# A state-space and experts layer on one core: five states' products on GpSimd in place of seven

## The chip, the cores and the metric

The kernel runs on one core of one Trainium2 chip. The metric is the device time of one execution in microseconds (us); less is better. A verdict compares medians of several executions.

The engines are named as the profile names them: PE is TensorE's matmul side and PEld its weight loads, DVE is VectorE, ACT is ScalarE, POOL is GpSimd, SP is SyncE. On-chip memory is SBUF; the matmul results stand in PSUM, 128 partitions in both.

## What is computed

The input x holds 16 samples of 512 tokens with 128 features, in float32. Four blocks follow each other, each with a layer norm ahead of it and a residual sum behind: a Mamba block, a product-key experts block, a small gated recurrence, and the experts block again. The change lies in the Mamba block. There, with 256 inner channels d and 16 states n, every token t does

```
dA = exp(delta[t, d] * A[d, n])
h[d, n] = dA * h[d, n] + (delta[t, d] * u[t, d]) * B[t, n]
y[t, d] = sum over n of h[d, n] * C[t, n]
```

The experts block looks up 8 rows of a table for every token, takes a dot product of each with the token, a GELU, and a weighted sum.

## The kernel before, in words

**Stages.** One sample is worked on at a time in three overlapping stages: PRE of sample i+1 (layer norm, convolution, delta), CORE of sample i (the 16 states), and POST of samples i-1 and older (the rest of the Mamba block, both experts blocks and the recurrence). An iteration has 64 slots (`TURN`), four for each state: the slots 4n to 4n+3 are those of state n. Every engine walks through the same slots in program order. Beside the states, the stages of PRE and POST are put into slots by the table `SLOTS` (L57), which was written out by hand; an engine does what its slot holds and waits on semaphores where an operand is not there.

**One state in CORE.** PE spreads row n of C over all partitions into the PSUM tile `c_ps` (L767) and row n+1 of B into `b_ps` (L758), both in the first slot of state n, C first. DVE scans along the tokens (L1352): it reads the decays `dA` from SBUF, which ACT made three states earlier (L1026), and the fed values from PSUM, and writes the state to one of the four buffers `hp`. Then DVE multiplies du by `b_ps` (the feed of state n+1, L1336). The state is then multiplied by C in place. For most states DVE does this in the third slot, with `c_ps` as its second operand (L1362). For the states in `POOL_STATES` POOL does it in the first slot (L1481). It cannot read PSUM, so ACT first copies `c_ps` to the SBUF tile `c_row` (L1043), of which there is one (`NCR` is 1). PE sums the product over the states in `ysum` (L783): two multiplications by the identity for each state, which the trace shows as four records.

**What the table of states also sets.** `SUM_AT` (L225) is the state in whose first slot PE sums state n: n+1 for a DVE state, n+2 for a POOL state, at most 15. The sums stand behind the spreads of C and B in that slot. `c_used` (L609) is what frees `c_ps` for the next C: for a POOL state ACT's copy, for a DVE state DVE's product. PE waits for it in `spread_c` (L761). Behind `spread_c` in PE's order stands `spread_b`, which the next feed on DVE waits for. A scan waits until the sum of the state that used its buffer is done (L1349).

**Other work around the change, by slot.** On PE: the two large convolutions (L809) in slots 15 and 19, the two plain ones (L812) in slots 25 and 27, a layer-norm product (`pe_ln_c`) in 16, the experts' sums (L716) in 25, 34, 45 and 59, the experts' similarities (L679) in 35, 38, 44, 46, 49, 51, 54 and 56. On DVE: the experts' dot products (L1265, eight in one group) in slots 11, 16, 22, 32, 36, 44, 53 and 59, the experts' weights `coef` (L1272) in 8, 21, 35 and 51, the maxima and masks (L1232, L1239) and the indices (L1248 to L1257), the first of them in slot 42. On POOL: indirect fetches of expert rows (L1466), four to a part, in slots 9, 10, 16, 25 (three parts), 35, 36, 43 and 47 (two parts each), 61 and 62. In POOL's program a product comes ahead of the fetches of its slot.

```python
POOL_STATES = (1, 3, 5, 7, 9, 11, 13)
DVE_STATES = tuple(n for n in range(NS) if n not in POOL_STATES)
SUM_AT = [min(n + 1 + (n in POOL_STATES), NS - 1) for n in range(NS)]
```

Of the kernel before, what the change touches and what calls it, by code (L numbers as in the profile page):

```python
# [218 lines left out]
}  # L219


POOL_STATES = (1, 3, 5, 7, 9, 11, 13)
DVE_STATES = tuple(n for n in range(NS) if n not in POOL_STATES)

SUM_AT = [min(n + 1 + (n in POOL_STATES), NS - 1) for n in range(NS)]  # L225
SUM_ORDER = sorted(range(NS), key=lambda n: (SUM_AT[n], n))
# [29 lines left out]
def at(b, per, k=0):  # L256

    return b * per + (k + 1)
# [30 lines left out]
def build(nc, A):  # L289
    with ExitStack() as ctx:  # L290
# [312 lines left out]
        def multiplied(c, n):  # L603

            if n in POOL_STATES:
                return pool_read, at(c, len(POOL_STATES), POOL_STATES.index(n))
            return read_out, at(c, len(DVE_STATES), DVE_STATES.index(n))

        def c_used(c, n):  # L609

            if n in POOL_STATES:
                return c_kept, at(c, len(POOL_STATES), POOL_STATES.index(n))
            return multiplied(c, n)
# [953 lines left out]
```

## Time and profile before

| what | value |
| --- | --- |
| median of 3 executions | 2184.6 us |
| lowest, highest | 2182.73, 2188.92 us |
| the profiled execution | span 2189.7 us, its own time not listed beside it |
| busy share of PE, DVE, ACT, POOL | 77%, 81%, 70%, 62% |

The span is the time from the first to the last instruction of the one execution that was profiled. Busy time of an engine counts its data instructions, not waits, branches and semaphore work. An instruction that starts and then cannot get its operands counts as busy: its duration in the trace is longer than that of others of its kind. Square brackets behind an instruction in a timeline give the idle time of its engine ahead of it and what ended it. Not all matmul records of `c_ps` are in the trace.

### The profile page before, as it was taken

To read this page: it belongs to the slowest core of one execution; us is meant where nothing else is said; L and a number is where in the kernel's file an instruction comes from. 1 tells how busy PE (TensorE), PEld (TensorE's weight loads), DVE (VectorE), ACT (ScalarE), POOL (GpSimd) and SP (SyncE) were. 2 spreads that over 40 slices of the span, in tenths; PEclk is the share of its full clock that TensorE was granted. 3 is DMA by queue.
4 is the path that set the end of the run, shared out by engine and by line. 5 is a ranking of instruction groups with operands and counts; after the bars stand their busy time and mean duration, and the time that the engine had idled before them with its cause. 6 is when DMAs were issued, how large, how long until landed. Compare 5 with 4: busy or idle time off the path is not lost. (4 is left out here: it accounts for less than half of the span.)

```text
span 2189.7 us, 24718 instructions
## 1 busy us (share of the span) xinstructions
PE 1681.9 (77%) x6097; PEld 937.5 (43%) x6186; DVE 1767.2 (81%) x4204; ACT 1543.5 (70%) x3276; POOL 1355.7 (62%) x1209
## 2 busy tenths in 40 slices
PE   4887878787887978888888879788878877754562
PEld 2332435354544545454544444454544444433342
DVE  3898989798988989898898989898889997733331
ACT  4565868587877868787878778777877765554542
POOL 0226463667776667677676676677677776566554
PEclk8898989998999999998999989999989988886776
DMA  2001120222222222222222222322222222233222
GB/s 54 0 10 56 32 65 23 62 66 75 82 80 77 70 84 68 82 77 65 84 80 77 73 84 68 84 68 74 76 75 82 72 80 73 71 87 92 78 82 71
DMA packets 79901, 151.06 MB, mean 69 GB/s; under 512 B 20584, under 2 KB 46592, under 8 KB 79680
## 3 DMA queue, kind: packets, MB, share of 16 engines
q0 software_dynamic: 49152, 134.28, 21.3%
q1 hardware_dynamic: 29344, 14.65, 2.4%
q8 instruction: 61, 1.00, 0.2%
q14 instruction: 96, 0.79, 0.1%
q10 hardware_dynamic: 1248, 0.34, 0.1%
HBM read 145.01 MB, written 4.19 MB: 68 GB/s over the span
## 5 line engine op out<-in xcount | busy, mean ns | idle before, releaser
L1466 POOL DMA_INDIRECT rows<-in_experts,index x1024 | 980.8, 958 | 477.6 <-issue 363.2
L1352 DVE TENSOR_TENSOR_SCAN hp<-dA,fed_ps 128x1024 f32<-128x1024 f32 x256 | 582.3, 2275 | 7.0 <-issue 5.8
L783 PE MATMUL ysum<-hp,ident 128*128 128x512 f32 x1024 | 503.9, 637 | 16.0 <-DVE hp L1362 9.0
L1481 POOL TENSOR_TENSOR hp<-hp,c_row 128x1024 f32<-128x1024 f32 x112 | 263.9, 2356 | 279.2 <-ACT c_row L1043 179.8
L1336 DVE TENSOR_TENSOR fed_ps<-du,b_ps 128x1024 f32<-128x1024 f32 x256 | 313.4, 1224 | 58.4 <-remote 26.3
L1026 ACT ACTIVATE dA<-delta,decay 128x511 f32<-128x511 f32 x512 | 334.8, 711 | 15.8 <-issue 7.9
L1005 ACT ACTIVATE rows<-rows,coef 128x128 f32<-128x128 f32 x1024 | 311.0, 390 | 19.2 <-DVE coef L1272 19.2
L783 PEld LDWEIGHTS ysum<-hp,ident 128*128 128x128 f32 x1024 | 215.0, 211 | 251.3 <-issue 218.5
L1265 DVE CUSTOM_DVE_ANT_0 rows<-rows,xn 128x128 f32<-128x128 f32 x1024 | 261.5, 318 | 51.7 <-DMA rows<-in_experts,index 51.2
L933 ACT ACT_TABLE_LOAD x218 | 279.7, 1283 | 8.8 <-PEq L543 5.0
L716 PE MATMUL bank<-rows,ident 128*128 128x256 f32 x1024 | 247.4, 397 | 34.0 <-ACT rows L1005 33.4
L716 PEld LDWEIGHTS bank<-rows,ident 128*128 128x128 f32 x1024 | 206.0, 202 | 67.2 <-ACT rows L1005 34.6
L679 PE MATMUL bank<-w_sim,xnT 128*128 128x512 f32 x256 | 175.1, 773 | 70.3 <-ACT x L998 30.4
L1232 DVE TENSOR_REDUCE top<-bank 128x16 f32<-128x512 f32 x128 | 87.4, 683 | 116.2 <-PE bank L679 72.6
L1362 DVE TENSOR_TENSOR hp<-hp,c_ps 128x1024 f32<-128x1024 f32 x144 | 174.7, 1214 | 2.4 <-PE c_ps L767 0.8
L758 PE MATMUL b_ps<-split,pick 128*128 128x512 bf16 x251 | 106.4, 424 | 36.8 <-DVE fed_ps L1336 21.0
L998 ACT ACTIVATE x<-bank 128x256 f32<-128x256 f32 x64 | 24.3, 379 | 151.4 <-remote 70.8
L986 ACT ACTIVATE flip<-bank 128x1024 bf16<-128x1024 bf16 x64 | 65.1, 1017 | 84.9 <-PE bank L690 57.9
L809 PE MATMUL bank<-xrT,w_taps 128*128 128x512 f32 x256 | 118.1, 604 | 3.4 <-ACT ucs L1117 2.5
L1239 DVE TENSOR_TENSOR mask<-bank,top 128x512 bf16<-128x512 f32 x128 | 88.6, 692 | 13.4 <-DVE top L1232 0.5
L1043 ACT ACTIVATE c_row<-c_ps 128x512 f32<-128x512 f32 x112 | 65.6, 586 | 46.7 <-PE c_ps L767 28.2
L767 PE MATMUL c_ps<-split,pick 128*128 128x512 bf16 x185 | 78.2, 423 | 18.7 <-DVE hp L1362 14.3
(182 smaller groups left out, 2357.6 us busy)
## 6 DMA issues: line engine op xcount, KB each, us to landing
rows<-in_experts,index POOLq DMA_INDIRECT x1024
x_in<-in_x SPq DMA_DIRECT2D x16, 256.0 KB
x_res<-in_x SPq DMA_DIRECT2D x16, 256.0 KB
y<-x SPq DMA_DIRECT2D x16, 256.0 KB
rows<-in_taps SPq DMA_DIRECT2D x1, 512.0 KB
rows<-in_wq_t SPq DMA_DIRECT2D x1, 512.0 KB, 5.3
rows<-in_in_proj_t ACTq DMA_DIRECT2D x1, 256.0 KB
rows<-in_key_t SPq DMA_DIRECT2D x1, 128.0 KB, 5.2
```

The source lines that it names most:

```text
L679: nc.tensor.matmul(bank[k][:], e.xnT[:, t * P:(t + 1) * P], w_sim[:], start=True, stop=True).then_inc(e.sim, 1)
L716: mm = nc.tensor.matmul(total, ident[:], e.rows[:, tiles, h, P:2 * P], start=False, stop=(h == HEADS - 1), skip_group_check=True)
L783: mm = nc.tensor.matmul(ysum[:, j, :], ident[:], hp[:, BUFFER[k], j, :], start=(k == SUM_ORDER[0]), stop=(k == SUM_ORDER[-1]))
L933: act.preload_act_table_set(name)
L1005: op = nc.scalar.activation(row, row, ACT.Copy, scale=e.coef[:, t, h:h + 1])
L1026: op = nc.scalar.activation(dA[:, n % NDA, j, 1:T], delta[q][:, j, 1:T], ACT.Exp, scale=decay[:, j, n:n + 1])
L1265: op = nc.vector.tensor_tensor_reduce(row, row, e.xn[r][:, t, :], 1.0, 0.0, ALU.mult, ALU.add, e.dot[:, t, h:h + 1])
L1336: nc.vector.tensor_tensor(fed_ps[:], src[:], b_ps[:].to_broadcast([P, NH, T]), ALU.mult).then_inc(fed, 1)
L1352: nc.vector.tensor_tensor_scan(flat, dA[:, n % NDA, :, :].rearrange("p a b -> p (a b)"), fed_ps[:].rearrange("p a b -> p (a b)"), 0.0, ALU ...
L1362: nc.vector.tensor_tensor(state, state, c_ps[:].to_broadcast([P, NH, T]), ALU.mult).then_inc(read_out, 1)
L1466: pool.indirect_dma_start(e.rows[:, t, h, :], None, A["experts"], bass.IndirectOffsetOnAxis(ap=e.index[:, t, h:h + 1], axis=0)).then_inc(e ...
L1481: pool.tensor_tensor(state, state, c_row[:, k % NCR, :].unsqueeze(1).to_broadcast([P, NH, T]), ALU.mult).then_inc(pool_read, 1)
```

## The change

The tuple of states whose product POOL makes is shorter and spaced by three; everything that is derived from it follows.

```diff
-POOL_STATES = (1, 3, 5, 7, 9, 11, 13)
+POOL_STATES = (1, 4, 7, 10, 13)
 DVE_STATES = tuple(n for n in range(NS) if n not in POOL_STATES)
 
 SUM_AT = [min(n + 1 + (n in POOL_STATES), NS - 1) for n in range(NS)]
```

By these lines the products of states 3, 5, 9 and 11 go from POOL to DVE, those of 4 and 10 from DVE to POOL, and 1, 7 and 13 stay on POOL. In the slots of states 1, 3, 5, 7, 9, 11, 13 and 15 PE summed 1, 2, 2, 2, 2, 2, 2 and 3 states before. Now it sums in those of 1, 3, 4, 6, 7, 9, 10, 12, 13 and 15, and the numbers are 1, 2, 1, 2, 1, 2, 1, 2, 1 and 3.

## Rows read from the trace of the kernel before

**Rows 1.** The page's head and its part 1: busy time of each engine

```profile
span 2189.7 us, 24718 instructions
...
PE 1681.9 (77%) x6097; PEld 937.5 (43%) x6186; DVE 1767.2 (81%) x4204; ACT 1543.5 (70%) x3276; POOL 1355.7 (62%) x1209
```

**Rows 2.** Groups of instructions: count, busy us, mean ns, idle before

```profile
L783 PE MATMUL ysum<-hp,ident 128*128 128x512 f32 x1024 | 503.9, 637 | 16.0 <-DVE hp L1362 9.0
L1481 POOL TENSOR_TENSOR hp<-hp,c_row 128x1024 f32<-128x1024 f32 x112 | 263.9, 2356 | 279.2 <-ACT c_row L1043 179.8
...
L1362 DVE TENSOR_TENSOR hp<-hp,c_ps 128x1024 f32<-128x1024 f32 x144 | 174.7, 1214 | 2.4 <-PE c_ps L767 0.8
...
L1043 ACT ACTIVATE c_row<-c_ps 128x512 f32<-128x512 f32 x112 | 65.6, 586 | 46.7 <-PE c_ps L767 28.2
```

**Rows 3.** Busy time by window, summed over samples 4 to 14, first scan to first scan

```profile
sum 1340.80, PE 1111.93 PEld 626.38 DVE 1214.24 ACT 1062.75 POOL 935.48; mean PE 101.08 PEld 56.94 DVE 110.39 ACT 96.61 POOL 85.04
```

**Rows 4.** Busy time by window, same samples, from scan 4 to scan 8

```profile
sum 262.40, PE 261.51 PEld 148.24 DVE 255.73 ACT 244.06 POOL 155.47; mean PE 23.77 PEld 13.48 DVE 23.25 ACT 22.19 POOL 14.13
```

**Rows 5.** Timeline of PE, sample 12, states 4 to 8: start us, us

```profile
1446.14 0.38 PE L767 MATMUL c_ps<-split,pick 128*128 128x512 bf16 x1
...
1452.01 0.38 PE L758 MATMUL b_ps<-split,pick 128*128 128x512 bf16 x1
1452.22 3.60 PE L783 MATMUL ysum<-hp,ident 128*128 128x512 f32 x8
1455.65 0.38 PE L767 MATMUL c_ps<-split,pick 128*128 128x512 bf16 x1
...
1462.02 0.38 PE L758 MATMUL b_ps<-split,pick 128*128 128x512 bf16 x1
```

**Rows 6.** Timeline of DVE, sample 12, states 4 to 8

```profile
1444.72 0.27 DVE L1265 CUSTOM_DVE_ANT_0 rows<-rows,xn 128x128 f32<-128x128 f32 x1
...
1446.77 1.23 DVE L1336 TENSOR_TENSOR fed_ps<-du,b_ps 128x1024 f32<-128x1024 f32 x1 [0.29 <-PE b_ps L758]
...
1452.42 1.23 DVE L1336 TENSOR_TENSOR fed_ps<-du,b_ps 128x1024 f32<-128x1024 f32 x1
1453.56 1.78 DVE L1272 SCALAR_TENSOR_TENSOR coef<-score,act 128x16 f32<-128x16 f32 x1
...
1464.04 1.23 DVE L1336 TENSOR_TENSOR fed_ps<-du,b_ps 128x1024 f32<-128x1024 f32 x1
...
1466.38 2.25 DVE L1352 TENSOR_TENSOR_SCAN hp<-dA,fed_ps 128x1024 f32<-128x1024 f32 x1
```

**Rows 7.** Windows with `coef` (L1272) alone, 16 samples: states 5, then 8

```profile
sum 108.60, DVE 21.70; mean DVE 1.36
...
sum 118.10, DVE 24.86; mean DVE 1.55
```

**Rows 8.** Timeline of POOL, sample 12, states 5 to 8

```profile
1452.96 2.35 POOL L1481 TENSOR_TENSOR hp<-hp,c_row 128x1024 f32<-128x1024 f32 x1 [5.05 <-ACT c_row L1043]
1455.46 0.98 POOL L1466 DMA_INDIRECT rows<-in_experts,index  x1
...
1472.57 2.36 POOL L1481 TENSOR_TENSOR hp<-hp,c_row 128x1024 f32<-128x1024 f32 x1
```

**Rows 9.** Timeline of DVE, sample 12, states 10 to 13

```profile
1485.43 0.69 DVE L1239 TENSOR_TENSOR mask<-bank,top 128x512 bf16<-128x512 f32 x1
...
1488.91 0.19 DVE L1248 TENSOR_SCALAR bits<-bank 128x32 int32<-128x32 int32 x1 [0.46 <-PE bank L702]
...
1501.84 0.69 DVE L1232 TENSOR_REDUCE top<-bank 128x16 f32<-128x512 f32 x1 [3.09 <-remote]
...
1506.90 0.17 DVE L1272 SCALAR_TENSOR_TENSOR coef<-score,act 128x16 f32<-128x16 f32 x1
...
1512.28 2.64 DVE L1265 CUSTOM_DVE_ANT_0 rows<-rows,xn 128x128 f32<-128x128 f32 x1
```

**Rows 10.** Timeline of PE, sample 12, the sums in state 11's first slot

```profile
1489.24 4.93 PE L783 MATMUL ysum<-hp,ident 128*128 128x512 f32 x8
```

## The prediction

> **What bounds the kernel now.** The page's busy shares come first: DVE has the most, 1767.2 of 2189.7 us, PE follows with 1681.9 [rows 1]. A share over the whole span mixes the filling and the draining of the pipeline with its middle, so the second view is busy time by window over samples 4 to 14, which have all stages in flight. Eleven samples take 1340.8 us, 121.9 each; DVE is busy for 110.4 of these, PE for 101.1, POOL for 85.0 [rows 3]. DVE leads, with some 11.5 us of waits in each sample. The third view cuts a sample: from scan 4 to scan 8 (262.4/11 = 23.9 us) PE is busy for 23.8 and DVE for 23.3 [rows 4]. There both engines are full and neither can take more for nothing. The timelines show how they touch: B's spread for feed 6 ends on PE at 1452.01 + 0.38 = 1452.39, and the feed starts at 1452.42; feed 5 waited 0.29 us for its own [rows 5, 6]. So in this stretch PE ends last by a hair. Further on DVE waits openly, 0.46 us for the index of state 10 and 3.09 us for a maximum in state 12 [rows 9].
>
> Busy time of DVE also hides waits. In state 5, `coef` took 1.78 us and ended at 1455.34, with POOL's product, which ended at 1452.96 + 2.35 = 1455.31 [rows 6, 8]. Both its tensor inputs lie in SBUF. The dot product behind scan 13 took 2.64 us where another took 0.27 [rows 6, 9]. The scans, the feeds and DVE's own products, which read one input from PSUM, show no such stretch.
>
> **The change, part by part.** All numbers are for one full sample, against the profiled span of 2189.7 us; this is 5.1 us above the median of 2184.6, and I take this off at the end.
>
> *Work that moves.* Two products in each sample leave POOL: 32 of 2.356 us, 75.4 us. DVE gains 32 of 1.214 us, 38.8 us in all or 2.4 in a sample. ACT loses 32 copies of 0.586 us, 18.8 us [rows 2]. POOL and ACT are not what DVE and PE wait for in scans and feeds, so what they save counts as zero; should it count, it is in the fast rival. PE's matmuls are the same in number, but their sums move.
>
> *States 3 to 6.* DVE multiplies state 3 itself, 1.2 us ahead of scan 4, and no longer state 4. On PE the sum of state 3 moves from state 5's slot to state 4's, ahead of B's spread for feed 6. It is half of 3.60 us, 1.8 [rows 5]. PE has no gap there [rows 4], so feed 6 starts about 1.8 us late. DVE alone would be late by 0 to 2.4 us: product 4 on POOL can start once its C is copied, C's spread ends at 1446.52 [rows 5] and the copy takes 0.59, so from about 1447.1. The dots of that slot run 1.2 us later than before, from 1445.9 on for 1.7 us, and one of them can be caught for up to 2.36. I take PE's +1.8; ends 0 and +2.4.
>
> *Feed 6 to feed 8.* `coef` is free of product 5: 0.17 in place of 1.78 us [rows 6, 9]. But DVE's product 5 follows, and now PE's C for state 6 must wait for it, with B's spread for feed 7 and the sums queued behind. The product ends 1.23 + 0.17 + 1.21, about 2.5 us with overlaps, after feed 6 starts. From C's spread for state 6 (1455.65) to the end of B's spread for feed 8 (1462.40) PE needs 6.75 us [rows 5]; the sums of states 4 and 5, 3.60 us, now lie in between. So feed 8 comes 2.5 + 6.75 + 3.60 = 12.85 us after feed 6, against 1464.04 - 1452.42 = 11.62 before [rows 6]: +1.2. Ends: 0, where the sums overlap with waits on ACT, and +2.4, if that wait also costs PE its start. DVE alone would need 2.5, then dots of 1.8, two scans of 2.25, a feed and a product of 1.2 each, 11.2; so about 1.6 us of this is a new wait of feed 8.
>
> *State 8.* Before, product 7 ran late behind twelve fetches (1455.46 to 1472.57 [rows 8]) and stretched `coef`: 24.86 us over the eleven samples that have it there, of which eleven undisturbed ones at 0.17 would be 1.9, so 23.0 or 2.1 in each [rows 7, 9]. Now product 4 stands ahead of the four fetches of slot 16 (some 5 us, at most the 17.1/12 = 1.4 of those twelve for each); the twelve start near 1454.6 and end near 1471.7, 1 us earlier than before, and product 7 runs to 1474. DVE's scan 8 ends at 1468.63 + 3.0, so the dots behind it are caught at 1471.6 in place of `coef`: -2.1 + 1.8, I take -0.3; ends -2.1 and +0.3.
>
> *States 9 and 10.* Product 9 on DVE lies in a full stretch: +1.1 net of overlap. Product 10 goes to POOL, but the index behind it hangs on PE and ACT after the mask, from 1485.43 + 0.69 to 1488.91 [rows 9]; without the product DVE waits 1.6 us instead of 0.46. The removal gives 0; ends -0.5 and +0.6, the latter for the sum of state 9 that PE now has in state 10's slot.
>
> *States 11 to 13.* Product 11 adds 1.1 us. On the other side the two sums in state 11's slot, 4.93 us in this sample [rows 10], move to state 12's. The similarities behind them come earlier, and DVE's wait of 3.09 us goes. What is late next is the turn into the second experts block, which now stands behind the two sums in state 12, so most of the gain is lost before state 13. Net -1.2; ends -2.5 (all of the wait less product 11) and +1.2. The stretch behind scan 13 stays, 2.64 against 0.27; end -2.4.
>
> *Sum.* 1.8 + 1.2 - 0.3 + 1.1 + 0 - 1.2 = +2.6 us in each of eleven samples, 28.6. The other five are less full; I give them the two products less a little cover, 1.8 each, 9. Together +38: 2227.7 for such a profiled execution, less 5.1, **2222 us**.
>
> **Weighed against the trace.** The stretches of DVE cost what rows show, and only with two inputs in SBUF [rows 6, 9], so moving a product frees some of them and not 2.36 us each. The Trainium skill (Perfetto Trace Analysis, section Optimizing Scalar/DVE Operations) says that the two engines share a read port and that offloading from one to the other might not help. If every product on POOL cost DVE its whole length, this change would gain 75.4 - 38.8 = 36.6 us; the trace supports it for some products only.
>
> **The rivals.** *Faster, the stalls decide (0.15).* The place is products 7 and 13: if 7 starts clear of dots and `coef`, and 13 ends before the dots, DVE saves 19.5 us on `coef` of state 5 (21.70 less thirteen times 0.17) and 23.0 on that of state 8 [rows 7], and 11 x 2.4 = 26 behind scan 13. With 38.8 added this is -30, or 2155; with half of the stalls of 7 and 13, -5. It decides if PE's sums do not delay feed 6 and 8. For it: `coef` of state 5 is freed for certain. Against it: PE is full from scan 4 to scan 8. *No change (0.10).* DVE's 11.5 us of waits in a sample take up the 2.4 us: 2178 to 2191. Against it: the waits lie in states 10 to 15, and four products land elsewhere. *Slower by much more (0.20).* Every wait on the new order (C behind DVE's product) takes PE's turn, and the gain of state 11 is lost again behind the two sums in state 12: 1.8 + 2.4 + 0 + 1.1 + 0 + 0 = 5.3 in eleven samples and 2.4 in five, +70, or 2255. It decides if PE's busy time from scan 4 to scan 8 falls below that stretch by over 2 us. That the change doesn't do what it says: the derived tables follow the tuple, so only a state left on the wrong engine could be meant, and the counts would show it.
>
> **How the numbers follow.** My forecast has 0.55. The range reaches from just below the no-change case, and so into the part of the fast one where half of the stalls go, to just below the large one: 2174 to 2250. It leaves out some 0.1 on either side. The forecast's own is 2200 to 2240. A measurement of this kernel can tell about 0.3% from no change, 6.6 us. Slower: 0.55 + 0.20 = 0.75; same 0.10; faster 0.15.
>
> **What would show it.** Counts: 80 products on POOL, 176 on DVE, 80 copies on ACT. Right: feed 8 waits 1 to 2 us for B, PE waits for DVE's product 5 with C for state 6, scan 4 to scan 8 grows by some 3 us, the 3.09 us wait is gone and a shorter one stands behind it, `coef` of state 5 takes 0.17. Wrong: feed 8 starts without a wait, or a full sample takes less than 122 us.

## The result, and the profile after

The change makes the kernel slower by more than was forecast: **2275.3 us** (median, 2267.5 to 2290.6) against 2185.6 for the kernel before (2182.7 to 2188.9), four executions each. The ratio is 1.0423, 95% interval 1.0378 to 1.0469. That is +90 us where +38 was forecast, and outside the range. The profiled execution took 2290.6 us, 15 more than the median, so the views below show +99 rather than +90.

The page's head and its part 1, after, which answer to [rows 1]:

```profile
span 2288.9 us, 24654 instructions
...
PE 1719.0 (75%) x6097; PEld 936.5 (41%) x6186; DVE 1806.7 (79%) x4236; ACT 1530.1 (67%) x3244; POOL 1281.6 (56%) x1177
```

The groups of the page's part 5, after, which answer to [rows 2]; one more is the feed, whose idle time matters here, and its row of before stands last:

```profile
L783 PE MATMUL ysum<-hp,ident 128*128 128x512 f32 x1024 | 529.9, 659 | 14.4 <-DVE hp L1362 9.4
L1481 POOL TENSOR_TENSOR hp<-hp,c_row 128x1024 f32<-128x1024 f32 x80 | 188.4, 2355 | 430.9 <-ACT c_row L1043 334.4
L1336 DVE TENSOR_TENSOR fed_ps<-du,b_ps 128x1024 f32<-128x1024 f32 x256 | 313.1, 1223 | 101.4 <-PE b_ps L758 57.8
...
L1336 DVE TENSOR_TENSOR fed_ps<-du,b_ps 128x1024 f32<-128x1024 f32 x256 | 313.4, 1224 | 58.4 <-remote 26.3 <-PE b_ps L758 20.1 <-issue 5.2
```

The counts are those of the forecast: 80 products on POOL, and 32 more instructions on DVE. DVE's busy time grew by 39.5 us (1806.7 - 1767.2), just its 32 products of 1.21. The span grew by 99. So some 60 us are waits, and the feed's two rows name most of them: DVE now stands idle ahead of its feeds for 101.4 us instead of 58.4, and for B's spread alone for 57.8 instead of 20.1.

The windows tell where. Each row is one window of every sample, summed over samples 4 to 14. Before, in this order: scan 3 to 4, 7 to 8, 8 to 9, 9 to 11, 11 to 14; last, samples 0 to 3 whole:

```profile
sum 62.40, PE 59.25 PEld 36.04 DVE 60.45 ACT 61.74 POOL 51.34; mean PE 5.39 PEld 3.28 DVE 5.50 ACT 5.61 POOL 4.67
...
sum 52.00, PE 51.84 PEld 26.52 DVE 50.38 ACT 50.75 POOL 29.98; mean PE 4.71 PEld 2.41 DVE 4.58 ACT 4.61 POOL 2.73
...
sum 92.20, PE 65.18 PEld 46.35 DVE 92.20 ACT 67.40 POOL 76.16; mean PE 5.93 PEld 4.21 DVE 8.38 ACT 6.13 POOL 6.92
...
sum 163.00, PE 135.66 PEld 57.78 DVE 153.40 ACT 130.55 POOL 114.22; mean PE 12.33 PEld 5.25 DVE 13.95 ACT 11.87 POOL 10.38
...
sum 339.20, PE 258.43 PEld 132.91 DVE 272.62 ACT 244.47 POOL 229.25; mean PE 23.49 PEld 12.08 DVE 24.78 ACT 22.22 POOL 20.84
...
sum 391.60, PE 308.57 PEld 148.27 DVE 347.74 ACT 263.12 POOL 174.18; mean PE 77.14 PEld 37.07 DVE 86.94 ACT 65.78 POOL 43.54
```

After: the same six, and in third place scan 4 to 8, which answers to [rows 4]; ahead of all stand samples 4 to 14 whole, for [rows 3]:

```profile
sum 1403.70, PE 1140.69 PEld 626.35 DVE 1240.35 ACT 1054.73 POOL 884.48; mean PE 103.70 PEld 56.94 DVE 112.76 ACT 95.88 POOL 80.41
...
sum 73.30, PE 69.75 PEld 42.12 DVE 72.83 ACT 58.92 POOL 43.72; mean PE 6.34 PEld 3.83 DVE 6.62 ACT 5.36 POOL 3.97
...
sum 295.40, PE 265.07 PEld 144.26 DVE 257.22 ACT 229.37 POOL 178.93; mean PE 24.10 PEld 13.11 DVE 23.38 ACT 20.85 POOL 16.27
...
sum 80.20, PE 80.15 PEld 52.13 DVE 50.13 ACT 65.99 POOL 59.87; mean PE 7.29 PEld 4.74 DVE 4.56 ACT 6.00 POOL 5.44
...
sum 86.40, PE 65.96 PEld 44.94 DVE 86.40 ACT 59.47 POOL 66.47; mean PE 6.00 PEld 4.09 DVE 7.85 ACT 5.41 POOL 6.04
...
sum 188.40, PE 150.55 PEld 61.19 DVE 163.92 ACT 148.07 POOL 84.96; mean PE 13.69 PEld 5.56 DVE 14.90 ACT 13.46 POOL 7.72
...
sum 340.30, PE 252.51 PEld 130.25 DVE 284.35 ACT 247.76 POOL 207.68; mean PE 22.96 PEld 11.84 DVE 25.85 ACT 22.52 POOL 18.88
...
sum 422.40, PE 317.72 PEld 149.55 DVE 361.80 ACT 259.45 POOL 155.10; mean PE 79.43 PEld 37.39 DVE 90.45 ACT 64.86 POOL 38.78
```

Eleven full samples cost 62.9 us more (1403.7 - 1340.8), 5.7 each. Of these, scan 3 to 4 has 1.0 and scan 4 to 8 has 3.0, nearly all of it (28.2/11 = 2.6) between scans 7 and 8, where feed 8 stands; DVE is busy for 50.1 us there as before, so this is pure waiting. State 8 gives 0.5 back, states 9 and 10 take 2.3, and 11 to 13 end even. The four samples that fill the pipeline lost 30.8 us by themselves, 7.7 each.

PE's timeline, after, sample 12, states 5 to 7, and DVE's of the same stretch:

```profile
1532.85 0.38 PE L758 MATMUL b_ps<-split,pick 128*128 128x512 bf16 x1
1536.10 0.61 PE L767 MATMUL c_ps<-split,pick 128*128 128x512 bf16 x1 [2.87 <-DVE hp L1362]
1536.50 0.63 PE L758 MATMUL b_ps<-split,pick 128*128 128x512 bf16 x1
1536.92 4.87 PE L783 MATMUL ysum<-hp,ident 128*128 128x512 f32 x8
...
1547.45 0.38 PE L758 MATMUL b_ps<-split,pick 128*128 128x512 bf16 x1
```

```profile
1533.61 1.22 DVE L1336 TENSOR_TENSOR fed_ps<-du,b_ps 128x1024 f32<-128x1024 f32 x1
1534.74 0.17 DVE L1272 SCALAR_TENSOR_TENSOR coef<-score,act 128x16 f32<-128x16 f32 x1
1534.82 1.22 DVE L1362 TENSOR_TENSOR hp<-hp,c_ps 128x1024 f32<-128x1024 f32 x1
...
1547.86 1.23 DVE L1336 TENSOR_TENSOR fed_ps<-du,b_ps 128x1024 f32<-128x1024 f32 x1 [3.27 <-issue]
```

PE idles 2.87 us with C for state 6, until DVE has read C of state 5; the sums of states 4 and 5 then take 4.87 us instead of 3.60, and feed 8 waits 3.27 us. (The bracket names no releaser for this wait; B's spread ends at 1547.83, 0.03 us before the feed starts.) The windows of this stretch show why the sums are longer (columns: time, busy time of PE, PEld, DVE, ACT, POOL, then the clock granted to PE, the DMA engines' share and GB/s):

```profile
1530.00:1533.20 3.20, 3.15 (x8) 1.14 (x7) 3.18 (x6) 2.98 (x4) 2.29 (x4) 1.00 0.27 82
1533.20:1536.10 2.90, 0.03 (x2) 0.01 (x1) 2.90 (x6) 2.90 (x7) 2.29 (x3) 0.99 0.45 124
1536.10:1541.80 5.70, 5.70 (x11) 2.65 (x12) 5.59 (x19) 2.52 (x9) 2.48 (x4) 0.70 0.24 76
1541.80:1548.00 6.20, 6.20 (x25) 4.38 (x25) 2.93 (x3) 4.29 (x12) 4.68 (x6) 1.00 0.28 85
```

PE was busy for 0.03 of 2.90 us, and in the next 5.7 us the granted clock was 0.70 on average: part of this stretch ran at 1.2 GHz, the lower of the two levels, and the rest at 2.4. In seven of the eleven samples feed 8 waits 3.3 us in this manner, in the other four 1.6 us, with the sums at 3.60. The Trainium skill (TensorE: Matmul & The Clock Gate, section "HAM oscillation — how this bites in real kernels") describes a kernel in which PE waits between its bursts of matmuls and every next burst starts at the lower clock. This trace agrees for seven of the eleven pauses, with 4.87 against 3.60 us in sample 12, and not for the other four.

What became of the stretches of DVE under POOL's products: the three groups that hold them, before and then after.

```profile
L1265 DVE CUSTOM_DVE_ANT_0 rows<-rows,xn 128x128 f32<-128x128 f32 x1024 | 261.5, 318 | 51.7 <-DMA rows<-in_experts,index 51.2 <-issue 0.5
...
L1272 DVE SCALAR_TENSOR_TENSOR coef<-score,act 128x16 f32<-128x16 f32 x64 | 56.3, 880 | 19.2 <-ACT act L993 16.6 <-issue 2.7
...
L1216 DVE SCALAR_TENSOR_TENSOR off<-mv,rs 128x4 f32<-128x4 f32 x48 | 17.5, 365 | 8.7 <-ACT rs L940 8.1 <-issue 0.6
```

```profile
L1265 DVE CUSTOM_DVE_ANT_0 rows<-rows,xn 128x128 f32<-128x128 f32 x1024 | 299.8, 356 | 63.8 <-DMA rows<-in_experts,index 63.1 <-issue 0.6
...
L1216 DVE SCALAR_TENSOR_TENSOR off<-mv,rs 128x4 f32<-128x4 f32 x48 | 25.8, 538 | 8.4 <-issue 7.8 <-ACT rs L940 0.6
...
L1272 DVE SCALAR_TENSOR_TENSOR coef<-score,act 128x16 f32<-128x16 f32 x64 | 14.9, 233 | 19.1 <-ACT act L993 17.8 <-issue 1.3
```

`coef` got 41.4 us back, the dots lost 38.3 and `off` 8.3. Fewer products on POOL caught about as much DVE time as before in these three groups; what is caught only changed its name.

### The profile page after: what moved, and what is told of

Same layout as the page of the kernel before. It is cut to its first block and busy times, and to the rows that moved or that the text cites. A ratio compares the mean times of both kernels' runs of the same rounds, so it can differ in the third digit from the quotient of the medians.

```text
span 2288.9 us, 24654 instructions
## 1 busy us (share of the span) xinstructions
PE 1719.0 (75%) x6097; PEld 936.5 (41%) x6186; DVE 1806.7 (79%) x4236; ACT 1530.1 (67%) x3244; POOL 1281.6 (56%) x1177
## 5 line engine op out<-in xcount | busy, mean ns | idle before, releaser
L783 PE MATMUL ysum<-hp,ident 128*128 128x512 f32 x1024 | 529.9, 659 | 14.4 <-DVE hp L1362 9.4
L1481 POOL TENSOR_TENSOR hp<-hp,c_row 128x1024 f32<-128x1024 f32 x80 | 188.4, 2355 | 430.9 <-ACT c_row L1043 334.4
L1336 DVE TENSOR_TENSOR fed_ps<-du,b_ps 128x1024 f32<-128x1024 f32 x256 | 313.1, 1223 | 101.4 <-PE b_ps L758 57.8
L1265 DVE CUSTOM_DVE_ANT_0 rows<-rows,xn 128x128 f32<-128x128 f32 x1024 | 299.8, 356 | 63.8 <-DMA rows<-in_experts,index 63.1
L783 PEld LDWEIGHTS ysum<-hp,ident 128*128 128x128 f32 x1024 | 222.3, 218 | 250.5 <-issue 214.0
L679 PE MATMUL bank<-w_sim,xnT 128*128 128x512 f32 x256 | 185.4, 816 | 93.5 <-ACT x L998 25.9
L716 PEld LDWEIGHTS bank<-rows,ident 128*128 128x128 f32 x1024 | 208.1, 204 | 67.8 <-ACT rows L1005 33.0
L1362 DVE TENSOR_TENSOR hp<-hp,c_ps 128x1024 f32<-128x1024 f32 x176 | 213.4, 1213 | 4.6 <-DVE hp L1352 1.4
L679 PEld LDWEIGHTS bank<-w_sim,xnT 128*128 128x128 f32 x256 | 50.3, 232 | 113.0 <-issue 37.5
```

Source lines behind the costliest of these rows:

```text
L679: nc.tensor.matmul(bank[k][:], e.xnT[:, t * P:(t + 1) * P], w_sim[:], start=True, stop=True).then_inc(e.sim, 1)
L716: mm = nc.tensor.matmul(total, ident[:], e.rows[:, tiles, h, P:2 * P], start=False, stop=(h == HEADS - 1), skip_group_check=True)
L783: mm = nc.tensor.matmul(ysum[:, j, :], ident[:], hp[:, BUFFER[k], j, :], start=(k == SUM_ORDER[0]), stop=(k == SUM_ORDER[-1]))
L1265: op = nc.vector.tensor_tensor_reduce(row, row, e.xn[r][:, t, :], 1.0, 0.0, ALU.mult, ALU.add, e.dot[:, t, h:h + 1])
L1336: nc.vector.tensor_tensor(fed_ps[:], src[:], b_ps[:].to_broadcast([P, NH, T]), ALU.mult).then_inc(fed, 1)
L1362: nc.vector.tensor_tensor(state, state, c_ps[:].to_broadcast([P, NH, T]), ALU.mult).then_inc(read_out, 1)
```

## The experiments

The theory after the result was that the order on PE costs the time: the sums that move with the tuple, the spread of C that waits for DVE's product, and the clock that falls while PE waits. The rival was the work that DVE is held up in. All runs are compared with the kernel before, run beside them (medians 2180 to 2186); "after" is the changed kernel. The first five take the change apart.

**The old slots of the sums, the new states** (after, with):

```diff
-SUM_AT = [min(n + 1 + (n in POOL_STATES), NS - 1) for n in range(NS)]
+SUM_AT = [min(n + 1 + n % 2, NS - 1) for n in range(NS)]
```

> The changed kernel, with PE's sums put back into the slots of odd states as before (products still on GpSimd for 1, 4, 7, 10, 13). Theory A, the order on PE: the wait of feed 8 in state 7 (about 43 us over all samples) comes from the two sums that now stand behind the wait for DVE's product 5, and PE's clock falls while it waits; without that the time falls by 35 to 50 us, to 2225 to 2240, and feed 8 waits under 0.5 us. Theory B, DVE's added products alone: the sums don't matter, 2265 to 2285.

Measured: 2241.1 us, ratio 1.0277 (1.0253 to 1.0301), just above the range of theory A. The moved sums cost 34 us of the 90. Scan 7 to 8 took 51.9 us over the eleven samples, as before the change, and feed 8 no longer waits.

**The same, with the states 1, 5, 7, 11, 13** (as above, and):

```diff
-POOL_STATES = (1, 4, 7, 10, 13)
+POOL_STATES = (1, 5, 7, 11, 13)
```

> Seven states as before, less 3 and 9: products on GpSimd for 1, 5, 7, 11, 13, sums in their old slots. What is left of the change is DVE's work, two products of 1.21 us in each sample, and the wait of C's spread for them. Theory A: 32 products of 1.13 us net, 36 us, less what waits hide: 2205 to 2225. Theory B: as the changed kernel, 2260 to 2285, since the number of DVE's products is the same.

Measured: 2214.9 us, 1.0144 (1.0102 to 1.0185). Taking states 3 and 9 away from POOL, with all else as before, costs +33; 32 products of 1.21 us are 39. To have 4 and 10 on POOL instead of 5 and 11 costs 26 more.

**One of these two at a time**, old slots of the sums, states 1, 4, 7, 11, 13 and 1, 5, 7, 10, 13:

> Products on GpSimd for 1, 4, 7, 11, 13, sums in their old slots. Between the runs five_odd (1, 5, 7, 11, 13; 2215) and sums_back (1, 4, 7, 10, 13; 2241) stands one step each for 4 in place of 5 and for 10 in place of 11. If ACT's copy of C for state 4, which stands ahead of its squares in slot 16 and so ahead of PE's layer-norm product, is what costs: 2230 to 2245. If it is state 10: 2210 to 2220.

> Products on GpSimd for 1, 5, 7, 10, 13, sums in their old slots. The other half of the step: 2210 to 2222 if state 4 costs the 26 us, 2230 to 2245 if state 10 does.

Measured: 2232.9 us, 1.0219 (1.0171 to 1.0266), and 2227.0 us, 1.0212 (1.0172 to 1.0253): +18 and +12 over the last kernel. Together they make 30 beside the 26, but the intervals span some 20 us each, so neither number is firm.

**The sums of states 3 to 6 alone in their old slots** (after, with):

```diff
-SUM_AT = [min(n + 1 + (n in POOL_STATES), NS - 1) for n in range(NS)]
+SUM_AT = [min(n + 1 + (n % 2 if n < 7 else n in POOL_STATES), NS - 1) for n in range(NS)]
```

> The changed kernel with the sums of states 3 to 6 alone put back (3 and 4 in state 5, 5 and 6 in state 7); those of 9 to 12 stay where the change has them. Theory A: the wait of feed 8 goes with them, and with it nearly all of the 33 us between the changed kernel (2275) and sums_back (2241): 2240 to 2252. Rival, the sums in states 10, 12 and 13 cost as much: 2255 to 2270.

Measured: 2247.8 us, 1.0313 (1.0258 to 1.0368). Of the 34 us of the sums, 27 lie in those of states 3 to 6. In this kernel scan 4 to scan 9 takes 32.2 us in a full sample, as in the kernel before, against 34.7 in the changed one. Some 7 us are left for the sums of 9 to 12; the interval overlaps that of the experiment with all sums back, so these 7 are not shown.

**Is it DVE held under POOL's products?** Both kernels with POOL's product cut to the first column of each half; the rest of it is left out:

```diff
-pool.tensor_tensor(state, state,
-                   c_row[:, k % NCR, :].unsqueeze(1).to_broadcast([P, NH, T]),
+part0 = state[:, :, 0:1]
+pool.tensor_tensor(part0, part0,
+                   c_row[:, k % NCR, 0:1].unsqueeze(1).to_broadcast([P, NH, 1]),
                    ALU.mult).then_inc(pool_read, 1)
```

> The changed kernel with GpSimd's products cut to the first column of each half, so that they can't hold up DVE's instructions with two inputs in SBUF; the rest of those products is left out. DVE's stretches behind products are about 109 us in all here and 109 in the kernel before. Theory A: those in state 4 are covered by PE, the rest come off: 2275 less 50 to 90, 2185 to 2225. Theory C, the stretches moved to worse places and are what makes the change slow: 2160 or less, and the distance to the kernel before with the same cut falls under 30 us.

> The kernel before with the same cut of GpSimd's products. Theory A: 2185 less 60 to 100, 2085 to 2125, so that the distance between the two cut kernels stays at 60 to 110 us. Theory C: 2130 or more, with the distance under 30.

Measured: 2212.5 us (1.0149; 1.0106 to 1.0192) for the changed kernel and 2106.0 (0.9665; 0.9629 to 0.9702) for the one before. The products' length costs the one 63 us and the other 76, but the distance of the two grew from 90 to 107. The cut also lets the sums have POOL's products earlier, so it takes away more than DVE's being held. But as the distance doesn't shrink with it, the slowdown as a whole doesn't come from DVE being held. Where the full products are there, they still set when scan 9 starts; the account of state 8 below shows it. The same cut with the old slots of the sums, at the states of the change and at 1, 5, 7, 11, 13:

> Sums in the slots of odd states as in the run sums_back, products on GpSimd for 1, 4, 7, 10, 13 cut to the first column of each half; the rest of those products is left out. It asks why the placement 1, 4, 7, 10, 13 with the old sums took 26 us more than 1, 5, 7, 11, 13. Theory S, GpSimd's products of 4 and 10: they stretch DVE's dots and offsets, and PE waits for them in the next slot: the distance between the two cut kernels falls under 10 us. Theory Q, the C spread that waits for DVE's product at other states: the distance stays at 20 to 30.

> Products on GpSimd for 1, 5, 7, 11, 13, sums in their old slots, and the same cut. It should lie 30 to 40 us above the kernel before with this cut, 2106, so at 2135 to 2145, if DVE's two products per sample cost the same with the stretches gone. Theory S: within 10 us of the run sums_back_short; theory Q: 20 to 30 below it.

Measured: 2168.4 us (0.9943; 0.9914 to 0.9973) and 2134.1 (0.9771; 0.9727 to 0.9815). The distance of 26 us between the two sets of states stays, at 34. So that distance isn't DVE under POOL's products either.

**Does the clock count?** After, with matmuls that add zero while PE would wait for C of state 6:

```diff
+nothing = sb("nothing", [P, P], BF16)
...
+nc.vector.memset(nothing[:], 0.0)
...
+if n == 6:
+    for _ in range(10):
+        nc.tensor.matmul(ysum[:, 0, :], nothing[:], split[q][:], start=False, stop=False,
+                         skip_group_check=True)
 spread_c(c, split[q], n)
```

> The changed kernel with ten multiplications by a tile of zeros, added into the sum on PE, between B's spread for feed 6 and the wait of C's spread for state 6 (one idle stretch of 2.9 us or more in each sample). Nothing is waited for less. Theory A with the clock: after that idle stretch the group of sums runs at half of the clock for a part (4.9 to 5.9 us in place of 3.60) and feed 8 waits 3.3 us or more in eleven of the samples; with PE busy there feed 8 waits 1.6 in all, and 15 to 30 us come off: 2245 to 2260. Rival, the long groups are due to something else (contention for the banks): no change or slower, 2270 to 2290.

Measured: 2273.3 us, 1.0438 (1.0411 to 1.0465), no gain that shows, where theory A had 15 to 30 us. But where it was placed it did its work. PE's timeline, sample 12, states 5 to 7:

```profile
1517.87 0.38 PE L760 MATMUL b_ps<-split,pick 128*128 128x512 bf16 x1
1518.09 2.32 PE L778 MATMUL ysum<-split,nothing 128*128 128x512 bf16 x10
1521.19 0.39 PE L769 MATMUL c_ps<-split,pick 128*128 128x512 bf16 x1 [0.78 <-DVE hp L1368]
...
1521.63 3.60 PE L789 MATMUL ysum<-hp,ident 128*128 128x512 f32 x8
```

The sums take 3.60 us again, in all eleven full samples. This kernel's windows of scan 7 to 8, then 8 to 9, samples 4 to 14:

```profile
sum 67.80, PE 67.80 PEld 42.45 DVE 50.19 ACT 56.39 POOL 50.66; mean PE 6.16 PEld 3.86 DVE 4.56 ACT 5.13 POOL 4.61
...
sum 96.80, PE 66.97 PEld 45.07 DVE 96.80 ACT 58.94 POOL 74.18; mean PE 6.09 PEld 4.10 DVE 8.80 ACT 5.36 POOL 6.74
```

State 7 gets 12.4 us shorter (80.2 to 67.8) and state 8 gives 10.4 of it back (86.4 to 96.8): DVE is full there, and its dots are held under product 7, whose time is set by the fetches that stand ahead of it on POOL, not by feed 8: it starts within 0.02 us of the last fetch's end in every full sample. So the fallen clock is real and costs 1.7 us where it falls, but most of that is taken back one state later. (The traces of all eleven samples lie 11.8 us apart, 1403.7 and 1391.9, but the changed kernel's is that of its slowest execution.)

**B's spread ahead of C's in every slot** (after, with the two calls exchanged):

```diff
-spread_c(c, split[q], n)
 if n + 1 < NS:
     spread_b(c, split[q], n + 1)
+spread_c(c, split[q], n)
```

> The changed kernel with B's spread ahead of C's in PE's order, in every slot. Theory A: B for feed 7 no longer waits for DVE's product 5, but the sums, the convolution and the experts' sum still stand behind it and ahead of B for feed 8, so feed 8 waits as before: 2255 to 2280. Rival, the wait of C's spread itself holds up B and that is the cost: 2235 or less.

Measured: 2258.7 us, 1.0362 (1.0344 to 1.0381). The feeds no longer stand behind C's wait in the same slot; the sums still do. Some 13 us come back by the ratios, 16 by the medians; the intervals just overlap, so this gain is likely and not shown.

**The price of one product more on DVE** (before, without state 5 on POOL, old slots of the sums; states 1, 3, 7, 9, 11, 13):

> The kernel before with one product less on GpSimd: 1, 3, 7, 9, 11, 13, all sums in their old slots. DVE gains 16 products of 1.13 us net, 18 us, and loses the stretch of the experts' weights behind product 5, 19.5 us in all. Theory A (DVE and PE both full from scan 4 to scan 8): C for state 6 now waits for DVE's product 5, with the old sums ahead of it on PE, so that nothing more is lost: 2170 to 2195. Rival, any product moved to DVE costs its 18 us: 2195 to 2210.

Measured: 2201.7 us, 1.0091 (1.0058 to 1.0124): +22 for 16 products, 1.4 us each, in the range of the rival and not of theory A. `coef` was freed (13.4 us in all, against 56.3 before), and nothing of the 19.5 us of state 5 showed in the time; the dots took 282.5 us instead of 261.5. This speaks against the fast rival, though C for state 6 now waits for DVE as well, and the run doesn't part the two.

**What makes states 4 and 10 a bad choice?** Old slots of the sums, states 1, 4, 7, 10, 13, and ACT's copies of C for 4 and 10 put behind the rest of their slots; then for 4 alone; then the copies as they were, with DVE's products 5 and 11 moved up directly behind the feed:

```diff
-if n in POOL_STATES:
+if n in POOL_STATES and n not in (4, 10):
     c, k = b[CORE], POOL_STATES.index(n)
...
+if CORE in has and part == 0 and n in (4, 10):
+    c, k = b[CORE], POOL_STATES.index(n)
...
+    nc.scalar.activation(c_row[:, k % NCR, :], c_ps[:, 0, :],
+                         ACT.Copy).then_inc(c_kept, 1)
```

```diff
-if CORE in has and part == 2 and n in DVE_STATES:
+if CORE in has and part == (1 if n in (5, 11) else 2) and n in DVE_STATES:
```

> The places 4 and 10 cost some 26 us over 5 and 11 with the odd sums (2241 against 2215). Theory K: ACT's copy of C for states 4 and 10 stands ahead of the squares of slot 16 and of the softplus of slot 40, and what PE wants from these comes late. With both copies behind the other work of their slots this kernel gives back half or more of the 26: 2213 to 2228; PE's layer-norm product of slot 16 starts about 0.6 us earlier against scan 4. Rival D: the price lies with DVE's products 5 and 11, which hold the next spread of C; the copies change nothing: 2236 to 2246. Rival P: the later copy makes POOL's product later, which is caught by more dots and delays the sum: slower than 2246.

> The same for state 4 alone. Theory K: about half of what both copies give, 2222 to 2236, and the rest of it by state 10. Rival D: 2236 to 2246. If both copies gain and this one nothing, the price is in state 10 alone.

> With the odd sums and places 1, 4, 7, 10, 13, DVE's products of states 5 and 11 stand directly behind the feed, ahead of the coef, the dots and the maxima of their slots. Rival D: the next spread of C is released earlier by what stood between, and 10 or more of the 26 us come back: 2215 to 2231. Theory K: 2236 to 2246, since little stands between the feed and the product there.

Measured: 2228.9 us, 1.0202 (1.0156 to 1.0248); 2229.6 us, 1.0216 (1.0184 to 1.0249); 2237.9 us, 1.021 (1.0146 to 1.0275). Against the 1.0277 of the kernel with the copies in front, the copy of state 4 alone gives back about 13 us (the intervals are apart, by little), and that of 10 adds nothing that shows. The products are unclear: their interval overlaps that of the kernel with the copies in front, and it also holds a gain larger than the copy's. PE's timeline shows what the copy does. With the copies in front, sample 12, behind C's and B's spreads of state 4:

```profile
1481.83 0.38 PE L758 MATMUL b_ps<-split,pick 128*128 128x512 bf16 x1
1483.80 0.49 PE L669 MATMUL bank<-w_y_ln,xnbT 128*128 128x128 f32 x2 [1.59 <-ACT x L957]
...
1485.69 3.60 PE L809 MATMUL bank<-xrT,w_taps 128*128 128x512 f32 x8
```

With the copies late:

```profile
1476.21 0.38 PE L758 MATMUL b_ps<-split,pick 128*128 128x512 bf16 x1
1476.94 0.49 PE L669 MATMUL bank<-w_y_ln,xnbT 128*128 128x128 f32 x2 [0.35 <-ACT x L957]
...
1478.83 3.60 PE L809 MATMUL bank<-xrT,w_taps 128*128 128x512 f32 x8
```

PE waits for ACT's squares 1.59 us or 0.35 (1.58 and 0.19 on average over the eleven samples), and the convolution behind, which B's next spread stands behind, starts 3.86 or 2.62 us after B's spread. Over the eleven samples scan 4 to 6 takes 164.7 us with the copies in front and 150.2 without, of which state 8 gives back 3.9 (86.5 to 90.4). What the place 10 costs, and the rest of the 26 us, stays open. In the changed kernel itself PE doesn't wait for the squares there in any of the eleven samples: the sum of state 3, which the change has moved into this slot, fills the time (1.88 us in sample 12), and the convolution starts 3.85 us after B's spread on average, as it does with the old slots and the copies in front. So the copy's 13 us are its price with the sums in their old slots; with the moved sums both delays lie over each other.

No version that does all of the work is faster than the kernel before.

## Why the prediction was wrong

The direction was right, and so was the mechanism ahead of feed 8. The sizes were not, and three steps failed: what DVE meets between feed 6 and scan 9, what is late next in states 9 to 13, and the samples that fill the pipeline.

- **Work that moves.** Right: DVE's products cost nearly their length (+33 for 32 in the second experiment, 39 by their duration), and what POOL saves counted as nothing.
- **States 3 to 6, forecast +1.8.** Scan 3 to 4 grew by 1.0, scan 4 to 6 by 0.4 (159.5 to 163.8 over eleven samples), +1.4 in all. The size was right, the reason only in part: DVE's product 3 lies in the first window, and in six of the eleven samples, 12 among them, feed 6 started when DVE was free, not when PE was. In the other five it waited 1.3 to 1.4 us for B's spread.
- **Feed 6 to feed 8, forecast +1.2.** This term was mis-sized: scan 6 to 8 grew by 2.6 (3.0 less 0.4). The step itself was right: C for state 6 waits for DVE's product 5, two sums stand behind, and feed 8 was to wait 1.6 us. It did, 1.6 us, in the four full samples in which the sums took 3.60. In the other seven they took up to 5.3, with the granted clock lowered after PE's idle 2.5 to 3 us, and the wait was 3.3. I had put 3.60 from [rows 5], a group behind a busy PE, into a place where PE comes from a pause. In the full samples this error was of no account for the time, though, since by scan 9 it is gone.
- **State 8, forecast -0.3.** Measured -0.5, and that was luck: it is +0.5 in the four samples with sums of 3.60 us, which are the case that was forecast, and -1.1 in the seven others, where state 8 gives back what feed 8 lost. From scan 6 to scan 9 the change costs 2.0 us in the four and 2.1 in the seven, against +0.9 forecast (1.2 - 0.3). Scan 9 goes by product 7 on POOL. In sample 12 before, it started at 1474.89, as that product ended (1472.57 + 2.36 [rows 8]), since `coef`, the last work ahead of it, was held until then; so it was in ten of the eleven samples. After, a dot is held in place of `coef`, and scan 9 comes 3.9 us behind the product's end, since the rest of the dots, feed 9 and DVE's product 8 still stand between. POOL, then DVE, after, sample 12:

```profile
1551.07 2.36 POOL L1481 TENSOR_TENSOR hp<-hp,c_row 128x1024 f32<-128x1024 f32 x1
```

```profile
1552.37 1.22 DVE L1265 CUSTOM_DVE_ANT_0 rows<-rows,xn 128x128 f32<-128x128 f32 x1
...
1557.35 2.27 DVE L1352 TENSOR_TENSOR_SCAN hp<-dA,fed_ps 128x1024 f32<-128x1024 f32 x1
```

  The distance from the product's end to scan 9 is 3.7 to 3.9 us in ten of the eleven samples, whether feed 8 waited 1.6 us or 3.3. The forecast had seen that a dot would be caught in place of `coef`, and priced the stretch alone, not the work behind it.
- **States 9 and 10, forecast +1.1.** Measured +2.3: 1.7 in state 9 and 0.6 in state 10. Product 9 is in with 1.2, and DVE's waits beside it grew by 0.5, most of it for a maximum behind PE's similarities; the sum had nothing for these. The removal of product 10, put at 0, came out at its upper end. The index starts 4.2 us after the mask on average instead of 3.6, so DVE only waits longer, in sample 12 for 1.39 us instead of 0.46. In that sample ACT's work on delta (L1142), which stands ahead of the index's step on ACT, waits 1.07 us for PE, where the sum of state 9 now stands in front: the reason that had been given for that end.
- **States 11 to 13, forecast -1.2.** Measured +0.1. The wait of 3.09 us did go, but 1.57 us in the same state took its place. State 11 lost 0.8, state 12 gained 1.7, and state 13 lost 1.0 again in waits for the maxima. DVE, after, sample 12:

```profile
1569.86 0.69 DVE L1239 TENSOR_TENSOR mask<-bank,top 128x512 bf16<-128x512 f32 x1
...
1573.69 0.19 DVE L1248 TENSOR_SCALAR bits<-bank 128x32 int32<-128x32 int32 x1 [1.39 <-PE bank L702]
...
1589.30 0.69 DVE L1232 TENSOR_REDUCE top<-bank 128x16 f32<-128x512 f32 x1 [1.57 <-PE bank L679]
```

  The loss behind the two sums of state 12 was named, "most of the gain", but -1.2 with a product of 1.1 books 2.3 of the 3.09 us all the same. The end of -2.5 was wrong by itself: all of the wait less the product is -2.0.
- **The other five samples, forecast 9 in all.** The worst step. The samples 0 to 3 took 30.8 us more and the last one about 6. "Less full" was taken to mean that work is hidden. But on DVE they are full enough (347.7 of 391.6 us before), and PE is emptier, so that in samples 2 and 3 it idles longer ahead of C for state 6 (4.53 us in sample 2) and its sums run slower behind it: 5.95 us there, and feed 8 waited 6 us. Over the four samples feed 8 waited 13.5 us, against 0.4 before; the rest of the 30.8 is not taken apart.
- **The sum.** 5.7 instead of 2.6 in each of eleven samples gives +63, not +29, and 37 instead of 9 for the rest.
- **The rivals.** The stalls brought no gain: `coef` of state 5 was freed as said, and the dots were caught instead. The Trainium skill (SBUF — State Buffer, section "Who interferes with whom") has it that a DVE instruction with two SBUF inputs contends with GpSimd's reads, and that one with at most one doesn't, outside DVE's 2-port modes. The groups agree, since dots, `coef` and `off` stretch and the products with `c_ps` stay at 1.21 us. So the question is what stands beside a product on POOL, more than how many products there are. "Slower by much more" came out, and its condition held: PE's busy time from scan 4 to scan 8 fell (295.4 - 265.1)/11 = 2.8 us below the stretch, where over 2 was the mark. It got 0.20, and even its 70 us were too few, since the five other samples had 2.4 each in it and took some 7.

What the runs show of the +90: about 33 for the two products on DVE, 27 for the sums of states 3 to 6, 7 (not shown by themselves) for those of 9 to 12, and 26 for 4 and 10 in place of 5 and 11, of which some 13 are the copy of C ahead of the squares of slot 16. These make 93, against 2181.6 us for the kernel before that ran beside the first of them. They are steps of one path from the kernel before to the changed one, so they add up by their nature, and another order of the steps could give other parts. The medians of the kernel before moved by up to 6.6 us between the runs, and the parts are hardly known better than that.

## What to carry to other kernels

A tuple that says which engine does a thing may also set where other engines do theirs: take the derived tables apart before you price the change, since here the order on PE cost as much as the work on DVE. Price a group on PE by rows in which PE comes from the same state, busy or paused, and look whether a later state takes the loss back. Where one engine's instruction holds another's, ask what is held and how much work stands behind it. And don't book a gain from a freed engine or a removed wait before you know what is late next: here, in states 10 and 12, the next wait stood within the same state.

## What was not expected of the hardware

- A pause of PE of 2.5 to 3 us was followed by slower matmuls in seven of eleven samples and not in four. Its length alone doesn't tell: in sample 10 it was 2.94 us and the eight matmuls behind it took 3.60; in sample 12, 2.87 us and 4.87. PE's timeline of sample 10:

```profile
1281.63 0.39 PE L767 MATMUL c_ps<-split,pick 128*128 128x512 bf16 x1 [2.94 <-DVE hp L1362]
...
1282.08 3.60 PE L783 MATMUL ysum<-hp,ident 128*128 128x512 f32 x8
```

- Ten matmuls that add zero, 2.32 us, kept the sums at 3.60 us in the full samples.
